# A transformer block on one core: the preparation ahead of self attention merged into it, its first loads split between two issuing engines

## What is computed

```
def _adaln(x, c, lw, lb, gw, gb, bw, bb):
    g = (c @ gw + gb)[:, None, :]
    bt = (c @ bw + bb)[:, None, :]
    return _ln(x, lw, lb) * (1.0 + g) + bt
attn_in = _adaln(x, cond, ln1_w, ln1_b, g1_w, g1_b, b1_w, b1_b)
x = _attn(attn_in, attn_in, sa_wq, sa_wkv, sa_wo, sa_bo) + x
cross_in = _adaln(x, cond, ln1_w, ln1_b, g1_w, g1_b, b1_w, b1_b)
ctx_n = _ln(context, ca_lnc_w, ca_lnc_b)
x = _attn(cross_in, ctx_n, ca_wq, ca_wkv, ca_wo, ca_bo) + x
ffn_in = _adaln(x, cond, ln2_w, ln2_b, g2_w, g2_b, b2_w, b2_b)
x = gelu(ffn_in @ ff_w1 + ff_b1) @ ff_w2 + ff_b2 + x
```

## Time and profile before

| | us |
|---|---|
| median of 3 runs | 2340.81 (2340.66 to 2345.96) |
| the profiled execution's own time | 2346.98 |
| its span in the trace | 2345.2 |
| load_constants and prepare of self attention | 0 to 68 |
| self attention | 68 to 1627 |
| cross attention and feed-forward | 1627 to 2345 |
| PE busy, share of the span | 2097.0, 89% |
| DVE busy | 1818.8, 78% |
| ACT busy | 1338.2, 57% |

### The profile page before, as it was taken

One profiled execution on the slowest core, in us unless ns is written; L12 is line 12 of the kernel. 1 busy time (PEld: TensorE's weight loads), 2 busy tenths in 40 slices (PEclk: granted clock), 3 DMA queues, 4 the chain that ended last, 5 costly groups with the idle time before them and its releaser, 6 DMA issues. The chain is left out here.

```text
span 2345.2 us, 37753 instructions
## 1 busy us (share of the span) xinstructions
PE 2097.0 (89%) x14744; PEld 908.7 (39%) x14744; DVE 1818.8 (78%) x2793; ACT 1338.2 (57%) x1710; POOL 127.6 (5%) x88
## 2 busy tenths in 40 slices
PE   3499999999999999999999999997368999983998
PEld 2133333335333334433333533334233444462566
DVE  6668998995989987789899589965768888836543
ACT  5366666664566675566666466662546666625221
POOL 2200000000000000000000000000400011113000
PEclk7689999999999999999999999998689999995999
DMA  5101001101111010110110111003323334334211
GB/s 173 57 28 47 31 34 43 36 34 46 46 46 36 30 46 28 46 55 28 46 38 28 46 46 47 28 20 92 87 86 113 112 123 124 115 87 119 73 36 36
DMA packets 107031, 140.30 MB, mean 60 GB/s; under 512 B 37025, under 2 KB 80111, under 8 KB 106863
## 3 DMA queue, kind: packets, MB, share of 16 engines
q1 hardware_dynamic: 106863, 138.01, 18.1%
HBM read 72.47 MB, written 13.11 MB: 36 GB/s over the span
## 5 line engine op out<-in xcount | busy, mean ns | idle before, releaser
L642 PE MATMUL sa_ps_o<-sa_probs,sa_v_pair 128*64 128x512 f32 x2048 | 534.3, 616 | 2.9 <-DVE sa_mx L897 2.9
L806 ACT ACTIVATE sa_probs<-sa_ps_s 128x1024 f32<-128x1024 f32 x512 | 495.9, 1025 | 29.8 <-PE sa_ps_s L629 29.8
L897 DVE CUSTOM_DVE_ANT_0 sa_rise<-sa_ps_t,sa_rise 128x512 f32<-128x512 f32 x504 | 327.9, 688 | 195.6 <-PE sa_ps_t L606 195.1
L910 DVE TENSOR_TENSOR sa_acc<-sa_acc,sa_probs 128x1024 f32<-128x1024 f32 x384 | 461.7, 1244 | 7.2 <-ACT sa_probs L806 7.2
L794 ACT ACTIVATE sa_rise<-sa_ps_t 128x1024 f32<-128x1024 f32 x252 | 257.7, 1022 | 250.2 <-PE sa_ps_t L599 250.2
L642 PEld LDWEIGHTS sa_ps_o<-sa_probs,sa_v_pair 128*64 128x64 f32 x2048 | 102.3, 135 | 248.9 <-issue 176.2
L622 PE MATMUL sa_ps_s<-sa_hi 64*128 64x512 f16 x1024 | 195.0, 377 | 0.0
L622 PE MATMUL sa_ps_s<-sa_lo,sa_hi 64*128 64x512 f16 x1024 | 194.9, 377 | 0.0
L622 PE MATMUL sa_ps_s<-sa_hi,sa_lo 64*128 64x512 f16 x1024 | 194.9, 377 | 0.0
L629 PE MATMUL sa_ps_s<-sa_m_line,sa_m_ones 64*128 64x512 f16 x1024 | 190.0, 378 | 4.2 <-DMA sa_m_line<-sa_m_rows 4.2
L780 ACT ACTIVATE sa_raw<-sa_ps_t 128x512 f32<-128x512 f32 x118 | 70.7, 599 | 104.5 <-PE sa_ps_t L338 104.5
(11 more groups left out here) (292 smaller groups left out, 4092.2 us busy)
## 6 DMA issues: line engine op xcount, KB each, us to landing
sa_swp<-sa_raw SPq DMA_DIRECT2D x128, 256.0 KB, 2.4
sa_inv<-sa_scratch SPq DMA_DIRECT2D x128, 128.0 KB, 2.9
ca_swp<-ca_raw SPq DMA_DIRECT2D x64, 256.0 KB, 2.3
ca_inv<-ca_scratch SPq DMA_DIRECT2D x64, 256.0 KB, 3.9
sap_xs<-in_x SPq DMA_DIRECT2D x4, 1024.0 KB, 7.2
sa_xr<-in_x SPq DMA_DIRECT2D x4, 1024.0 KB, 5.6
cap_xs<-x_after_self SPq DMA_DIRECT2D x4, 1024.0 KB, 7.4
x_after_cross<-ca_xr SPq DMA_DIRECT2D x32, 128.0 KB, 2.0
```

Source lines behind the costliest of these rows:

```text
L642: ins = pe.matmul(ps_o[rows(x), half(c)], v_pair[:, kt, rows(x)], probs[:, kt % 2, c, half(x)], start=(kt == 0), stop=(kt == NK - 1))
L806: act.activation(probs[:, kt % 2, c, :], ps_s[c][:, :], ACT.Exp, scale=float(DH) ** -0.5).then_inc(s_p, 1)
L897: dve.tensor_tensor_reduce(out=larger, in0=max_banks(j, t)[:, half(x)], in1=larger, scale=1.0, scalar=-3.0e38, op0=ALU.add, op1=ALU.max, a ...
L910: dve.tensor_tensor(acc[:, c, :], before, probs[:, kt % 2, c, :], ALU.add).then_inc(s_acc[c], 1)
```

## The change

- load_constants and the call of prepare for self attention are gone. What they did is part of self_attention's block; there is no barrier between.
- ACT issues the loads of the key and query weights (four pieces) and of both rotation tables as its first six instructions. SP issues the rest: x of sequence 0, conditioning and its matrices, columns, identity, value weights; behind the swaps of groups 0 and 1 the output weights, x of sequence 1, the bias and x for the residual.
- Only sequence 0 is normalised before the first projection. Its variances are turned into reciprocal roots on ACT by Ln and Exp (before: Sqrt on ACT and a reciprocal on DVE), then the Newton step. Key and query weights are split first; value and output weights later, between the rotations and the maxima of the first pair and after them.
- Sequences 1, 2, 3 are normalised within groups 0 to 3, 8 to 11 and 16 to 19: statistics in the first of the four (DVE, tiles 1 to 7), Ln and Exp in its tile 6, one normalising instruction in each tile of the second, and in tiles 3 and 6 of the third and fourth four transposes on PE, gamma and beta and the rounding on ACT, the remainder on DVE in the next tile. A projection of a new sequence waits for s_nlo.
- The shift is one block per key tile, after bases: four matmuls with 32 rows each (head by half) with m_line in four partition rows 32 apart, filled by one DMA. Both exponentials wait for that block.
- The swapped copy has one buffer in place of two, so SP waits in `swap` for the rotation before it.
- The maxima of group 0 use three PSUM banks; the two rotations of group 1 stand behind all maxima of group 0.
- The order of the pieces changes to key, query, value, output, also for cross attention.

```
@@ self_attention, TensorE
-                if shifted:
-                    shift(c)
-            def shift(c):
+            def shift():
                 for x in range(2):
-                    ins = pe.matmul(ps_s[c][:, half(x)], m_ones[rows(x), :], m_line[rows(x), half(c)],
-                                    start=False, stop=True)
+                    for c in range(2):
+                        quarter = slice(32 * (2 * x + c), 32 * (2 * x + c) + 32)
+                        ins = pe.matmul(ps_s[c][:, half(x)], m_ones[quarter, :], m_line[quarter, :],
+                                        start=False, stop=True)
...
+            pe.wait_ge(s_tab, 1)
+            pe.wait_ge(s_nlo, 4)
             for i in range(2):
+                pe.wait_ge(s_wlo, 2 * i + 2)
                 for c in range(2):
                     project(0, i, c)
...
                         for c in order(kt):
-                            scores(g, kt, c, shifted=(kt > 0))
-                        if kt == 0:
-                            pe.wait_ge(s_line, 32 * (g + 1))
-                            for c in order(kt):
-                                shift(c)
+                            scores(g, kt, c)
                     if j < G:
                         bases(j, kt)
+                    if g >= 0:
+                        if kt == 0:
+                            pe.wait_ge(s_line, 16 * (g + 1))
+                        shift()
...
+                    if norm_bank(g, kt) is not None:
+                        u, n = norm_bank(g, kt)
+                        pe.wait_ge(s_nxc, TT * (u + 1))
+                        transposes(u, n)
@@ self_attention, ScalarE
             def exponentials(g, kt, c):
-                act.wait_ge(s_st, score_count(g, kt, c))
+                act.wait_ge(s_st, NK * g + kt + 1)
...
+            def deviations(u):
+                act.wait_ge(s_nst, STEPS * u + 6)
+                act.activation(newton[:], var[:], ACT.Ln).then_inc(s_nln, 1)
+                act.wait_ge(s_nln, 2 * u + 1)
+                act.activation(rstd[:], newton[:], ACT.Exp, scale=-0.5).then_inc(s_nln, 1)
...
+            for n in range(4):
+                stage(act, n)
+            act.dma_start(ropeC[:], consts["cosines"]).then_inc(s_rope, 16)
+            act.dma_start(ropeS[:], consts["sines"]).then_inc(s_rope, 16)
+            deviations(0)
+            for q in range(TT):
+                normalise(0, q)
+            for n in range(4):
+                norm_high(0, n)
+            for n in range(4):
+                weights_high(n)
...
+                    if norm_of(g, 0) is not None and kt == 6:
+                        deviations(norm_of(g, 0))
+                    if norm_of(g, 1) is not None:
+                        normalise(norm_of(g, 1), kt)
+                    if norm_bank(g, kt) is not None:
+                        norm_affine(*norm_bank(g, kt))
+                        norm_high(*norm_bank(g, kt))
@@ self_attention, VectorE
             for t in range(TT):
                 maxima(0, t)
-                if t == 4:
-                    multiply(1, 1)
-                    rotated(1, 1)
-                if t == 6:
-                    multiply(1, 0)
-                    rotated(1, 0)
+            multiply(1, 1)
+            rotated(1, 1)
+            multiply(1, 0)
+            rotated(1, 0)
@@ self_attention, SyncE
             def swap(j, i):
                 sp.wait_ge(s_kq_r[i], 2 * j + 2)
+                before = {(0, 0): None, (0, 1): None, (1, 1): (0, 0), (1, 0): (0, 1)}.get((j, i), (j - i, 1 - i))
+                if before is not None:
+                    sp.wait_ge(s_rot[before[1]], before[0] + 1)
...
-                for x in range(2):
-                    sp.dma_start(m_line[DH * x:DH * x + 1, :], m_rows[TT * x:TT * x + TT, :]).then_inc(s_line, 16)
+                sp.dma_start(m_line[0:P:32, :], m_rows[:]).then_inc(s_line, 16)
```

More of the change, by code:

```diff
@@ L363, in output_projection, with self_attention @@
         product(t, range(KM), True, True).then_inc(s_y, 1)
-def self_attention(nc, consts, x_src, x_dst, bo, xT, wq, wk, wv, wo):
+def self_attention(nc, consts, x_src, x_dst, cond, norm, weights, bo, xT, wq, wk, wv, wo):
+    lnw, lnb, gw, gb, bw, bb = norm
+    xT_hi, xT_lo = xT
     NK = N // P
@@ L410, in self_attention @@
         turn = [ps_t[:, 0:HALF], ps_t[:, HALF:N]]
+        ps_gate = ps_s[0][:, 0:2 * KD * B].rearrange("p (i k b) -> p i k b", i=2, k=KD)
+        s_par = sem("s_par")
+        s_ident = sem("s_ident")
+        s_rope = sem("s_rope")
+        s_w = [sem(f"s_w{n}") for n in range(len(weights) // 2)]
+        s_whi = sem("s_whi")
+        s_wlo = sem("s_wlo")
+        s_gate = sem("s_gate")
+        s_tab = sem("s_tab")
+        s_nx = sem("s_nx")
+        s_nst = sem("s_nst")
+        s_nln = sem("s_nln")
+        s_nxc = sem("s_nxc")
+        s_ntr = sem("s_ntr")
+        s_nxn = sem("s_nxn")
+        s_nhi = sem("s_nhi")
+        s_nlo = sem("s_nlo")
         s_init = sem("s_init")
@@ L500, in late_norm, with stage @@
             return g >= PAIRS and g % PAIRS == 1
+        def stage(engine, n):
+            src = weights[n][0]
+            dst = staged[:, n, :]
+            if len(src.shape) == 3:
+                dst = dst.rearrange("p (a b) -> p a b", b=src.shape[2])
+            engine.dma_start(dst, src).then_inc(s_w[n // 2], 16)
         @block.sync
@@ L582, in project @@
                 b, pair = j // PAIRS, j % PAIRS
+                if pair == 0 and j >= PAIRS:
+                    pe.wait_ge(s_nlo, 4 * (next(u for u in NORMS if norm_batch(u) == b) + 1))
                 cols = slice(pair * P, (pair + 1) * P)
@@ L823, in _ @@
                     evacuate_kq(0, i, c)
+            weights_high(4)
+            weights_high(5)
             high(0, 0)
             high(0, 1)
-            rises(0, 0)
-            rises(0, 1)
+            for t in range(2):
+                rises(0, t)
             for c in range(2):
@@ L933, in residual, with variances, aggregate @@
                                          op0=ALU.mult, op1=ALU.add).then_inc(s_yr, 1)
+            def variances(u, tiles):
+                for t in tiles:
+                    ins = dve.bn_stats(stats[:, t, :], xs[:, t, :])
+                ins.then_inc(s_nst, TT // 2 // (TT // len(tiles)))
+            def aggregate(u):
+                dve.wait_ge(s_nst, STEPS * u + 4)
+                for t in range(TT):
+                    ins = dve.bn_aggr(mv[:, t, :], stats[:, t, :])
+                ins.then_inc(s_nst, 1)
+                dve.wait_ge(s_nst, STEPS * u + 5)
+                dve.tensor_scalar(var[:], mv[:, :, 1], EPS, None, ALU.add).then_inc(s_nst, 1)
@@ L941, in _ @@
+            variances(0, range(TT))
+            aggregate(0)
+            newton_step(0)
+            tables()
+            for n in range(4):
+                first_affine(n)
+            for n in range(4):
+                weights_low(n)
+            dve.wait_ge(s_rope, 32)
             for i in range(2):
```

236 lines of the change are left out of this document (185 added, 51 removed).

## The result

| | before | changed |
|---|---|---|
| median | 2341.12 us (4 runs, 2340.66 to 2345.96) | 2314.34 us (3 runs, 2310.86 to 2316.84) |
| ratio to before, 95% | | 0.988 [0.9857, 0.9902] |
| the profiled execution, its span | 2346.98, 2345.2 | 2316.84, 2315.0 |
| line of group 0 issued | 123.65 | 83.61 |
| last line issued | 1565.74 | 1535.79 |

A fourth execution of the changed kernel took 3034.85 us in a slow state, as did one execution each of the two kernels of experiments 10 and 11, and every median and ratio here leaves them out (with it this median would be 2315.59).

What follows compares the result with a forecast made beforehand. PE throughput was taken to bound self attention, latency the first 126 us. Terms -42 - 5.5 - 6 + 11 + 7.5 + 3 = -32 gave 2315 us profiled, 2309 against the median; range 2280 to 2332.

Steps and rivals of the forecast that it cites:

- The start: Before the first key projection: merged preparation and shared loads start it at 26.2 instead of 68.0, -42 us.
- rival 4: Norm work isn't hidden on DVE and ACT (+15), or ACT's loads all precede x (+5): 2324 us; chance 0.09.
- Before group 0: From the first projection to group 0's shift: rotations leave the maxima loop, -7.3, partly paid back behind it; net -5.5 us.
- The shift: In 256 key tiles: four 32-row matmuls run together in 0.22 us, with later exponentials; -0.2 a group, -6 for 31.
- rival 1: Shift: the quarter tiles go two at a time, +0.22 in each of 256 tiles, +56: 2365 us; chance 0.10.
- Rival 2: Shift: changing from 64 to 32 rows costs nothing, 256 x -0.09 = -24: 2285 us; chance 0.14.
- Transposes: Norms of sequences 1 to 3 inside self attention: twelve groups of four transposes on PE, not hidden, +11 us.
- Table loads: Groups 0, 8, 16: loads for Ln and Exp delay the next rise, which bases wait for, by 2.5 each; +7.5 us.
- DVE: Norms of sequences 1 to 3: 23 us of DVE work, mostly hidden where DVE idles; bounds 0 and 23, taken +3.

Runs made afterwards that it cites:

- experiment 10: Changed kernel plus all loads on SyncE, one table load, bases before differences, GpSimd's additions later, roundings before exponentials: median 2283.82 us, 0.9757 of the kernel before.
- experiment 11: The changed kernel unedited, timed again beside the kernel before: median 2313.61 us, ratio 0.9866.
- experiment 1: Changed kernel with ScalarE's six first loads issued by SyncE, in one queue behind x: 2308.87 us against 2316.84.
- experiment 2: Changed kernel with ScalarE keeping its six first loads but waiting for x before issuing them: 2306.80 us against 2316.84.
- experiment 6: Changed kernel with bases ahead of the next tile's differences in the loop before group 0: 2316.98 us against 2316.84.
- experiment 3: Changed kernel with the old shift back, 64-row pairs behind each half's scores and two line DMAs: 2314.51 us against 2316.84.
- Experiment 12: The kernel with all edits together, with the residual additions moved from GpSimd to VectorE: median 2268.17 us, 0.9679 of the kernel before.
- experiment 7: Changed kernel with one explicit load, first on ScalarE, of the table set holding both Ln and Exp: 2308.23 us against 2316.84.

## Why the prediction was right, and where it wasn't

Sign and size came out: 2314.3 for a forecast of 2309, inside the range. The mechanism came out too: latency taken off the start, partly paid back in the groups. How near the total came is in part luck, as two errors of opposite sign stand behind it (see the groups as a whole). Step by step, in the order of the sum:

- *The start, forecast -42, measured -37.2.* The mis-sized term is "x (1.05 MB) comes 1.05/0.41 = 2.6 late". I took an even sharing between the two issuers; experiments 1 and 2 put the delay at 5.7 (12.13 against 6.48 and 6.45). That lies between my 2.6 and the bound of 7.7, for which rival 4 had 5 us on top of the forecast. Behind x, 1.3 more were lost. 0.65 of it is VectorE's first remainder of the key weights, 1.86 instead of 1.21: GpSimd was at its last remainder of the activation until 28.50, and VectorE's ended 1.1 later, at 29.58. I had written that GpSimd's remainders run beside the rounding, and given them no price. The second remainder took its 1.21. About 0.5 are the transposes, whose last three groups end 2.9 after normalising does, for 2.4. The rest is small gaps between steps. The gate values came late ("which leaves them until about 17"; they began at 17.69, behind SP's stretched issues), but that cost nothing here: in experiment 1 they begin at 9.00, and the projection starts 18.7 after the statistics there as here.
- *Before group 0, forecast -5.5, measured -3.6* (-40.8 for the shift less the -37.2). Both stretches are longer than forecast, 23.1 for 22.6 and 13.5 for 12.6, and from the first projection to the first differences it now takes 18.1 us for 17.6. That the third bank wouldn't change the step of 2.45 was right, and experiment 6 shows what it is worth when the order does change.
- *The shift.* The text says "No row has 32 rows". That was an error of reading: cross attention of the kernel before has such a block. Its row (timeline of TensorE, kernel before):

```profile
1743.41 0.65 PE L1303 MATMUL ca_ps_s<-ca_m_line,ca_m_ones 32*77 32x512 f16 x4
1744.00 0.61 PE L338 MATMUL ca_ps_t<-xT_hi,ca_wq_hi 128*128 128x512 f16 x1
1744.40 0.54 PE L338 MATMUL ca_ps_t<-xT_hi,ca_wq_lo 128*128 128x512 f16 x1
```

  Four matmuls in 0.59 at a lower clock (granted 0.50 over 1730 to 1743 us, 0.56 over 1743.4 to 1744.9), with the change of shape in it, where one of 128 rows takes 0.40 (1744.00 to 1744.40): this row would have told against rival 1, whose 0.10 was too much. Measured are 0.22 for the four and about 0.10 for a change of shape; forecast were 0.22 and 0.09. By an estimate from the figure in "TensorE: Matmul & The Clock Gate", section "Measured speedup vs the span model", of the Trainium skill the four would take 0.29; this trace agrees with the full four as long as the change behind them costs 0.10, and 0.29 would leave it 0.04. The row of totals was misread as well: 1.07 is for eight matmuls of 32 columns (x8), as 1.98 is for eight of 64, so the ratio that I used stands. The ordinary group changed by -0.25 (-0.2), tile 3 to 4.03 (4.05), tile 1 to 5.96 (6.0), tile 5 by +0.10 (+0.15). Rival 2 is out: the change from 64 to 32 rows is paid. But the -6 for the stage isn't shown: undoing the shift (experiment 3) changed the 31 groups by 0.2 only. Of the 4.6 that the shift gains in sixteen of the groups, 3.4 are lost at the table loads of groups 8 and 16, and the others go up and down.
- *Transposes, forecast +11.* In sequence 1, groups 2 and 3 are 1.77 and 2.28 longer than an ordinary one (45.10 and 45.61 less 43.33), 4.1 for the 3.7 forecast. In sequences 2 and 3, groups 10, 11, 18 and 19 take 195.63 for 191.03 before, 4.6 more, or 5.6 with the 1.0 that the shift saves in them, for a forecast of 7.4. Together 9.7, but the second figure is loose: kernels with the same work there took 191.2 to 196.4 for these four groups. Experiment 12 is clearer. With GpSimd's additions gone, groups 3, 11 and 19 all take 45.25, 2.34 more than an ordinary 42.91, so the transposes are paid in sequences 2 and 3 as in 1. Where the changed kernel shows less (groups 18 and 19), part of them may lie inside TensorE's waits for VectorE; that is argued from the lengths and not shown.
- *Table loads, forecast +7.5, measured 6.6* by experiment 7, with the two loads and the gap where they were expected; the start's 1.3 turned out as 0.27. Part of the 6.6 is not the waiting but the lower clock behind it: groups 8 and 16 have the same wait of 1.91, and the one with the drop takes 0.95 more (47.80 for 46.85).
- *DVE, forecast +3.* Not measured by itself. Group 1, where ACT normalises, is 1.01 longer than an ordinary one; the groups with the statistics come to their ordinary length within 1.5 us once the table loads are gone (44.83 for 43.33).
- *The groups as a whole:* forecast -6 + 11 + 7.5 + 3 = +15.5, measured +10.1. The line of group 0 was forecast 7.5 too early, the groups 5.4 too long. The errors cancel in part, and the median is nearer to the forecast than the stages are.
- *Medians.* The sum was made between profiled executions, where -32 and the measured -30.2 nearly agree. The forecast of 2309 took off the 6.2 by which the kernel before lay above its median; the profiled execution of the changed kernel lay only 2.5 above its own. That difference, 3.7, is most of the 5.3 between 2309 and 2314.3.

What stays open: why the granted clock drops behind some waits of 2 to 3 us and not behind others. In groups 10, 11, 18 and 19 it differs between kernels that do the same there (behind the same wait of 2.10 in group 10, the granted clock over the next 6 us is 0.72 in the changed kernel and 1.00 in experiment 2, and the group takes 48.90 and 47.28), and in group 16 between two executions of one kernel (46.85 and 48.52). It is worth 1 to 3 us each time, and no edit here controls it.

## What to carry to other kernels

A second issuing engine for loads is no second road: put the load that everything waits for ahead in time, not merely in another queue. A block moved to a later place makes a wait; find the work on the waiting engine that could stand in it (here 0.4 us in every group), and price both halves of such an edit one by one. Set a single execution against a single one stage by stage, not by its total. Where an engine is late, look at what GpSimd does in the same microseconds before you believe the releaser that the wait names.

## What the runs showed of the hardware that was not expected

- With 3.15 MB issued by ScalarE in the first 5 us, x (1 MB, first in SP's queue at 0.73) came 5.7 us later, and SP's issue of one 256 KB matrix took 6.37 us instead of 0.91 (experiment 1).
- VectorE's whole-row float32 products and sums beside GpSimd's float32 addition took 3.36 and 3.25 us instead of 1.22 (experiment 6), and a pair of sums 5.09 instead of 2.36 (experiment 10, one by one 1.80 and 3.37). Each of these operations, and the key weights' first remainder in the changed kernel (1.86 for 1.21), ended 1.1 us after GpSimd's operation beside it did. Its maxima, with one operand in PSUM, kept their 0.69 (changed kernel, from 68.22 on, with GpSimd at work from 67.72 to 72.4).
- Behind one wait of TensorE of 1.91 us the granted clock was 0.76 over 480 to 486 us, and eight values took 2.79 us for 1.98. Behind the same wait in group 16 it stayed at 1.00 in one execution (values 1.94) and fell to 0.81 in another (3.62).
- Four matmuls of 32 rows and 512 columns and the change of shape behind them take 0.33 us, which fits 0.22 for the four together and about 0.10 for the change; the change ahead of them costs 0.10 as well.
